# Attention over a sequence of 32 in a fused block: one head's attention matrix stationary over four tiles, its result copied out and transposed back

## The reference

```python
q, k, v = mn @ Wq, mn @ Wk, mn @ Wv          # (N, L, H, C) after a reshape, mn the layer norm of x
g = sigmoid(mn @ Wg + bg)
att = softmax(einsum('slhc,tlhc->sth', q, k) * scale, axis=1)
o = einsum('sth,tlhc->slhc', att, v) * g
t = t + o.reshape(N, L, H * C) @ Wo + bo
```

## Time and profile before

| what | us |
|---|---|
| median of 3 runs | 1113.27 |
| profiled execution | 1112.62 |
| its span | 1110.9 |
| TensorE busy in the span | 900.8 (81%) |
| VectorE busy | 629.0 (57%) |
| ScalarE busy | 469.7 (42%) |
| GpSimd busy | 412.6 (37%) |
| mean granted clock of TensorE, share of 2.4 GHz | 0.886 |

### The profile page before, as it was taken

One profiled execution on the slowest core, in us unless ns is written; L12 is line 12 of the kernel. 1 busy time (PEld: TensorE's weight loads), 2 busy tenths in 40 slices (PEclk: granted clock), 3 DMA queues, 4 the chain that ended last, 5 costly groups with the idle time before them and its releaser, 6 DMA issues. The chain is left out here.

```text
span 1110.9 us, 24437 instructions
## 1 busy us (share of the span) xinstructions
PE 900.8 (81%) x8576; PEld 536.1 (48%) x8576; DVE 629.0 (57%) x1435; ACT 469.7 (42%) x841; POOL 412.6 (37%) x525
## 2 busy tenths in 40 slices
PE   4276599999997899798888259384999999999960
PEld 4135377777776566577666213031333333333320
DVE  1035477777884566368687834141555555555533
ACT  1023366666664344342331025141555555555530
POOL 0000255555553010003666653645444444444450
PEclk9685799999998899898996569696999999999995
DMA  6704400000002960000000211120111111111007
GB/s 121 86 20 118 81 11 11 10 9 9 9 5 85 340 209 2 2 2 14 23 22 23 59 30 31 33 44 20 42 43 42 42 42 38 40 41 40 22 1 227
DMA packets 107325, 57.02 MB, mean 51 GB/s; under 512 B 76261, under 2 KB 101697, under 8 KB 107264
## 3 DMA queue, kind: packets, MB, share of 16 engines
q1 hardware_dynamic: 89728, 45.56, 17.2%
q0 software_dynamic: 9088, 8.55, 2.5%
q10 hardware_dynamic: 8448, 2.10, 0.9%
HBM read 26.02 MB, written 28.97 MB: 50 GB/s over the span
## 5 line engine op out<-in xcount | busy, mean ns | idle before, releaser
L1571 DVE TENSOR_TENSOR norm_T<-norm_T,bank 114x512 f32<-114x512 f32 x234 | 154.2, 684 | 212.4 <-ACT norm_T L1374 146.9
L1279 PE MATMUL bank<-ex_xt,ex_w 64*114 64x512 f32 x936 | 233.7, 629 | 31.7 <-DVE norm_T L1571 24.5
L1165 POOL DMA_INDIRECT chosen_out<-ex_out,ex_id x156 | 155.2, 995 | 228.1 <-DVE ex_out L1561 189.7
L1374 ACT ACTIVATE norm_T<-bank 114x512 f32<-114x512 f32 x234 | 139.5, 598 | 129.9 <-PE bank L1279 90.4
L1157 POOL DMA_INDIRECT slot_x<-rows,slots x128 | 124.9, 976 | 117.9 <-DVE slots L1485 54.1
L1279 PEld LDWEIGHTS bank<-ex_xt,ex_w 64*114 64x114 f32 x936 | 78.7, 180 | 133.2 <-issue 127.6
L1289 PE MATMUL bank<-norm_T,ex_w 114*64 114x512 f32 x468 | 112.4, 616 | 0.0
L460 POOL TENSOR_TENSOR probs<-shifted,win_rden 128x512 f32<-128x512 f32 x64 | 66.7, 1043 | 104.2 <-DVE win_rden L650 97.5
L1289 PEld LDWEIGHTS bank<-norm_T,ex_w 114*64 114x64 f32 x468 | 30.9, 140 | 78.0 <-issue 64.1
L636 DVE TENSOR_REDUCE win_max<-ps_s 128x8 f32<-128x512 f32 x64 | 43.9, 685 | 36.6 <-PE ps_s L500 36.6
L1367 ACT ACTIVATE norm_T<-bank 128x512 f32<-128x512 f32 x39 | 23.3, 597 | 89.5 <-issue 59.2
(11 more groups left out here) (250 smaller groups left out, 1484.7 us busy)
## 6 DMA issues: line engine op xcount, KB each, us to landing
slot_x<-blank SPq DMA_DIRECT2D x1, 17028.0 KB, 56.3
ex_x<-slot_x SPq DMA_DIRECT2D x39, 132.0 KB
ex_x<-slot_x SPq DMA_DIRECT2D x39, 128.0 KB
w_in<-in_L_ffn_w_dram SPq DMA_DIRECT2D x24, 168.0 KB
chosen_out<-ex_out,ex_id POOLq DMA_INDIRECT x156
wlocal_in<-in_L_conv_w_local_dram SPq DMA_DIRECT2D x2, 1152.0 KB, 7.8
norm_T<-in_x_dram SPq DMA_DIRECT2D x16, 128.0 KB
residual<-in_x_dram SPq DMA_DIRECT2D x4, 512.0 KB, 7.4
```

What stands on the lines that cost most here:

```text
L1165: eng.indirect_dma_start(s.chosen_out[:, :], bass.IndirectOffsetOnAxis(ex_id[k % 4][:, j:j + 1].bitcast(U32), 0), out[k % 4][:, j, :], Non ...
L1279: eng.matmul(ps[c % DEEP][0:HCHUNK, :], w13[par][halves(i), c * HCHUNK:(c + 1) * HCHUNK], xt[par][halves(i), :], start=True, stop=True).th ...
L1374: eng.activation(act[c % DEEP], ps_1[c % DEEP][0:HCHUNK, :], ACT.Silu).then_inc(act_n, 1)
L1571: eng.tensor_tensor(h[par][:, c, :], act[c % DEEP], ps_3[c % DEEP][0:HCHUNK, :], ALU.mult).then_inc(h_n, 1)
```

## The change

`attend` swaps its operands. For each of 8 heads it holds `att_w` of the head stationary (128 by 128) and moves v of four tiles through it at once (4 by 32 columns), 8 matmuls. The result has tokens on partitions, so it has to be turned: ScalarE copies both banks `ps_o` to SBUF (`av_o`, two copies of 128 by 512 for each group), and a new function `turn_o` transposes the eight blocks of 128 by 128 into the banks `ps_g`, from which the tanh has read the gates by then. `gated` reads `ps_g` instead of `ps_o`.

With that the order changes. `turn_o(g-1)` stands at the start of step g on TensorE. `gates(g)` waits until `gated(g-1)` has read both banks, where it waited for the tanh before. On VectorE `gated(g-1)` opens step g (it was `gated(g)` behind `norm`), `norm` and `shifted` come next, and `residual(g-1)` behind them. On ScalarE the two copies stand behind the tanh and ahead of all pieces for the router. A semaphore of the experts stage gets another name (`done_n`), nothing else there changes.

```diff
+        o = [tmp(f"av_o{i}", [P, GROUP, P]) for i in range(2)]
...
                 def gates(g):
-                    wait(eng, gc_n, 2 * g)
+                    wait(eng, og_n, 2 * g)
...
                 def attend(g):
                     eng.wait_ge(va_n, 2 * g + 2)
+                    wait(eng, oc_n, 2 * g)
                     for m in range(2):
-                        wait(eng, og_n, 2 * g - 1 + m)
+                        for i in range(4):
+                            hd = 4 * m + i
+                            last = eng.matmul(ps_o[m][:, :].rearrange("p (t n) -> p t n", t=GROUP)[:, :, i * D:(i + 1) * D], s.att_w[:, place(hd), :],
+                                              v[g % 2][:, :, hd * D:(hd + 1) * D], start=True, stop=True)
+                        last.then_inc(o_n, 1)
+
+                def turn_o(g):
+                    eng.wait_ge(oc_n, 2 * g + 2)
+                    eng.wait_ge(gc_n, 2 * g + 2)
+                    for m in range(2):
                         for t in range(GROUP):
-                            for i in range(4):
-                                hd = 4 * m + i
-                                last = eng.matmul(ps_o[m][i * D:(i + 1) * D, t * P:(t + 1) * P], v[g % 2][:, t, hd * D:(hd + 1) * D],
-                                                  s.att_w[:, place(hd), :], start=True, stop=True)
-                        last.then_inc(o_n, 1)
+                            last = eng.transpose(ps_g[m][:, t * P:(t + 1) * P], o[m][:, t, :], s.ident[:, :])
+                        last.then_inc(ot_n, 1)
...
                 for g in range(STEPS):
+                    if 1 <= g <= GROUPS:
+                        turn_o(g - 1)
                     if g < GROUPS:
                         values(g)
                         gates(g)
...
                             eng.activation(gate[g % 2][:, m, :], ps_g[m][:, :], ACT.Tanh, bias=s.bg[:, m:m + 1], scale=0.5).then_inc(gc_n, 1)
+                        for m in range(2):
+                            eng.wait_ge(o_n, 2 * g + m + 1)
+                            wait(eng, ot_n, 2 * (g - 1) + m + 1)
+                            eng.activation(o[m][:, :, :], ps_o[m][:, :].rearrange("p (t n) -> p t n", t=GROUP), ACT.Copy).then_inc(oc_n, 1)
...
                 def gated(g):
                     for m in range(2):
-                        eng.wait_ge(o_n, 2 * g + m + 1)
+                        eng.wait_ge(ot_n, 2 * g + m + 1)
...
-                        eng.scalar_tensor_tensor(og[g % 2][:, m, :], gate[g % 2][:, m, :], 1.0, ps_o[m][:, :], ALU.add, ALU.mult).then_inc(og_n, 1)
+                        eng.scalar_tensor_tensor(og[g % 2][:, m, :], gate[g % 2][:, m, :], 1.0, ps_g[m][:, :], ALU.add, ALU.mult).then_inc(og_n, 1)
...
                     if 1 <= g <= GROUPS:
-                        residual(g - 1)
+                        gated(g - 1)
                     if chunk(g, 7) is not None:
                         slots(chunk(g, 7))
                     if chunk(g, 5) is not None:
                         shifted(chunk(g, 5))
+                    if chunk(g, 3) is not None:
+                        norm(chunk(g, 3))
+                    if 1 <= g <= GROUPS:
+                        residual(g - 1)
                     if chunk(g, 2) is not None:
                         center(chunk(g, 2))
-                    if chunk(g, 3) is not None:
-                        norm(chunk(g, 3))
-                    if g < GROUPS:
-                        gated(g)
-                    if chunk(g, 2) is not None:
                         spread(chunk(g, 2))
```

## The result

The changed kernel takes 1165.55 us (median of 4 runs, 1161.95 to 1168.65), the kernel before 1113.14 (4 runs, 1110.09 to 1114.11): a ratio of 1.0475 (95% interval 1.0437 to 1.0512). The prediction was 1146 with a range to 1166, so the sign and the chain that was forecast held, and the size was 19.6 us short, at the upper end of the range. The profiled execution took 1161.95 us, 49.3 more than the one of before, with a span of 1160.2.

What follows compares the result with a forecast made beforehand. TensorE paced the first steps; later, instruction waits and TensorE's low clock lengthened steps. The last residual 42.2 us later, less 9.1 given back, put 33.1 on 1112.62: 1145.7, the median 0.65 above, 1146 us; range 1126 to 1166.

Steps and rivals of the forecast that it cites:

- The chain: Routing stage: one chain from gated to the next gated, 7.6 us without router work, 12.6 in odd steps, 10.6 in even.
- The clock: TensorE at 1.2 GHz after idling in the odd step: project and turn cost each following even step 2.6 us more.
- The stalls: TensorE's waits for instructions inside attend, 14.5 us before, go away because 128 instructions become 48 with the transposes.
- the same work in the same order: Tail from the last residual to the experts, 36.15 us before: taken as unchanged.
- The stalls stay and move: Waits for instructions hit whatever runs during sends, up to 14.5 us, and 9.1 in the tail: 1162 us, chance 0.18.
- Given back: Start of the experts stage: the 9.1 us that the first expert lost during chunk 5's sends fall away.
- The clock stays up: TensorE's idle time in the routing stage doesn't lower its clock, 14.7 us fall out: 1132 us, chance 0.20.
- Faster: VectorE alone bounds the routing stage's second stretch, no engine waits for the chain, about 9 us gained: 1104 us, chance 0.07.
- no change: What the chain delays was waited for anyway, and the experts' freedom from sends pays it all: 1113 us, chance 0.03.

Runs made afterwards that it cites:

- without sends: Changed kernel with GpSimd's sends held back until the last table and eight row buffers instead of six: 1277.01 us; the kernel before, treated the same way, 1224.34 us.
- the runs with products in the wait: Changed kernel with five unread products ahead of gates in even steps from 6 on: 1150.81 us; also with the router ahead of ScalarE's copies: 1134.03 us.
- the order written anew: Changed kernel, copies and transposes kept, with values one group ahead, attend directly behind the transposes, and ScalarE's copies of the result first: 1133.43 us, ratio 1.0159.
- gates first: The order written anew with gates of a group ahead of project of the last one on TensorE: 1159.55 us, ratio 1.0375.
- values last: The order written anew with gates ahead of project and the next group's values behind both: 1162.22 us, ratio 1.0391.
- The run with pauses for chunk 5: Changed kernel with GpSimd's pauses between the sends of chunks 0 to 4 made for chunk 5 too: 1161.36 us, ratio 1.0401.

## Why the prediction was right and wrong

**The chain** was right. Steps 1 to 3 take 7.62, 8.76 and 7.62 us (7.6, 8.9 and 7.6 predicted), and without sends an odd step takes 12.46 us (12.6 predicted). That step 6 starts at 510.30 (510.1 predicted) is in part luck: the first gated came 0.56 us early and step 5 took 13.65 us instead of 12.6, since its values, ahead of gates, ran at 1.2 GHz. Taking its parts apart moved the time the way the chain says: the exponential and the square ahead of the copies (23.9 us of the stage), and attend with copies and transposes beside VectorE's pieces (33.4 us, 248.3 - 214.9).

Two terms of the sum failed, the clock and the stalls.

**The clock** in even steps was mis-sized. The step that failed is "I charge these 2.6 us to each following even step": it took project and turn alone, because the earlier trace rows show those two, behind a wait that stood ahead of project. In the changed kernel the wait stands ahead of gates, so gates ran at 1.2 GHz too (2.01 instead of 0.95 us), and a part of attend (2.5 to 3.6 us busy without sends, 2.2 charged). Even steps without sends took 14.81 us instead of 13.2, five times 1.6 = 8.0 us.

**The stalls** were not gone; the forecast put them at nothing in the steps, since the change "takes away the waits for instructions", and at nothing in the tail. With sends an odd step took 13.34 us instead of 12.46, an even one 14.94 instead of 14.81, 5.1 us in five pairs. The tail, called "the same work in the same order", took 41.4 us instead of 36.15; without sends it is 36.1 up to the last table (653.91 to 689.99), with them 40.95. Together that is some 10 us, more than the clock's 8.0. The rival "The stalls stay and move", the second in the list, had this mechanism and, at 1162, was nearer than the forecast, in part by luck: it had 16 us for the stalls and nothing for the longer even steps. Attend no longer has such waits, and other engines have more of them than without sends. By the Trainium skill, page "Runtime: NRT & Kernel Launch", section "Instruction fetch mechanics", fetches of instructions are mostly hidden. The trace agrees where no sends run: with the late sends no wait without a releaser is left on ScalarE or VectorE up to the changed kernel's last table. Beside sends the routing stage lost 9.7 us. That these waits are fetches is read from the absence of another releaser and is not shown.

**Given back** were 10.8 us for 9.1 predicted: the first expert, as said, ran nearly without gaps (0.18 us at most) and gave 9.45. Where the other 1.3 us come from is open.

Together: even steps 5 * (14.94 - 13.2) = 8.7, odd steps 5 * (13.34 - 12.6) = 3.7, tail 5.2, less 1.7 given back more, 15.9 of the 16.3 us by which the profiled execution missed the sum (1161.95 against 1145.7). The other 3 us are that the median lies 3.6 us above the profiled execution, not 0.65.

**The rivals.** "The clock stays up" is refuted by 0.77 and by the runs with products in the wait. "Faster" and "no change" needed an order without this chain; the order written anew is the nearest to one and is still 1.6% slower, by its first steps of 8.35 us and its later pairs. No run here that turns the result beats the kernel before; the one that is 0.5% faster leaves the turning out.

## What to carry to other kernels

A product with cheaper operands is paid by the layout of its result: price the way back (copies, transposes, and where they stand in each engine's order) before the product. Where two engines wait for each other in turns, an added copy costs what is queued behind it, so put it behind everything for which the other engine waits, or move the work that it copies so far ahead that it waits for nothing. And read a wait of TensorE together with all that runs behind it: if the engine that it waits for waits for TensorE next, the low clock lengthens both.

## What the runs showed of the hardware

- Useless work in TensorE's wait gained time in three kernels. With gates first, 3.4 us of products in each of five even steps took 22 us out of the stage (241.5 to 219.2, 3.1 of them in the tail), and project behind the wait ran at 2.4 GHz (2.00 us instead of 3.56).
- In the order written anew project took 2.00 us behind 0.68 and 0.75 us of idle time, 2.84 behind 2.83 and 3.68 behind 5.88 and 7.43. The eight transposes behind 1.44 us took 1.06 us once and 1.74 another time; with gates first, project took 3.56 us behind 3.93 us and gates. So the length of a wait alone doesn't tell at which clock the work behind it runs.
- In the tail of the changed kernel VectorE fell into a slow manner of single instructions. In the last choose nine of them had 0.24 to 1.18 us of idle time ahead, with its own last result as releaser (timeline of VectorE):

```profile
688.70 0.23 DVE L1466 TENSOR_TENSOR rt_work<-rt_probs,rt_best 128x64 f32<-128x64 f32 x1 [0.49 <-DVE rt_best L1465]
689.40 0.22 DVE L1467 SCALAR_TENSOR_TENSOR rt_work<-rt_work,rt_number 128x64 f32<-128x64 f32 x1 [0.48 <-DVE rt_work L1466]
690.11 0.22 DVE L1468 TENSOR_REDUCE rt_small<-rt_work 128x8 f32<-128x64 f32 x1 [0.49 <-DVE rt_work L1467]
```

They start 0.70 us apart, where the same instructions start 0.26 apart without sends. This one choose took 9.5 us (685.49 to 694.95) instead of 5.3, most of what the tail lost. It is no single accident: the last choose took 9.5 us with gates first and 9.7 with values last too, the other two kernels with a long tail, while no choose of the other twelve runs took more than 5.5. In all three the end of chunk 5's sends, made without pauses, falls into this choose (the last send of the changed kernel starts at 690.76 us). The run with pauses for chunk 5 has its last choose at the same time of the span (from 690.6 us) and doesn't show it. The cause stays open.
